# One block of a fused attention and feed-forward kernel: a maximum and its transpose taken one step earlier, four row transposes moved, clips interleaved

## The reference, cut to what matters

```
def _ln(x, g, b):                       # layer norm over the 512 features
    m = jnp.mean(x, axis=-1, keepdims=True)
    v = jnp.mean((x - m) ** 2, axis=-1, keepdims=True)
    return (x - m) * jax.lax.rsqrt(v + EPS) * g + b
h = _ln(x, pw_g[pathway_ids], pw_b[pathway_ids])
h = _ln(h, cp_g[compartment_ids], cp_b[compartment_ids])
t = _ln(x, tm_g[time_steps], tm_b[time_steps])
m, n, r = x + (one row each from three small conditioning networks)
s = _ln(x, ms_g[scale_type], ms_b[scale_type])
w = softmax(aw)
cat = concatenate([w[0]*h, w[1]*t, w[2]*m, w[3]*n, w[4]*r, w[5]*s])
u = _ln(silu(cat @ int_W1 + int_b1) @ int_W2 + int_b2, int_g, int_be)

def _L0_ffn_ref(lhs, rhs):              # lhs is u, rhs is 512 x 512
    lhs_scale = max(|lhs|, over a row) / 127
    rhs_scale = max(|rhs|, over a column) / 127
    q_lhs = clip(round(lhs / lhs_scale), -127, 127)
    q_rhs = clip(round(rhs / rhs_scale), -127, 127)
    return (q_lhs @ q_rhs) * lhs_scale * rhs_scale
out = x + _L0_ffn_ref(u, rhs)
```

## Time and profile before

| quantity | value |
|---|---|
| median of 3 runs | 1724.21 us (1722.79 to 1724.4) |
| the profiled execution | 1724.23 us |
| its span, first to last instruction | 1722.2 us |
| matrix engine busy | 1711.0 us, 99% |
| VectorE, ScalarE, POOL busy | 1249.2, 882.0, 728.7 us |
| granted clock of the matrix engine, mean | 0.998 |
| first block of the last stage | from 1208.65 to 1272.38 us of the span |

### The profile page before, as it was taken

One profiled execution on the slowest core, in us unless ns is written; L12 is line 12 of the kernel. 1 busy time (PEld: TensorE's weight loads), 2 busy tenths in 40 slices (PEclk: granted clock), 3 DMA queues, 4 the chain that ended last, 5 costly groups with the idle time before them and its releaser, 6 DMA issues. The chain is left out here.

```text
span 1722.2 us, 23029 instructions
## 1 busy us (share of the span) xinstructions
PE 1711.0 (99%) x7749; PEld 1385.2 (80%) x7749; DVE 1249.2 (73%) x1842; ACT 882.0 (51%) x1306; POOL 728.7 (42%) x642
## 2 busy tenths in 40 slices
PE   9999999999999999999999999999999999999998
PEld 7888888888888888888888888778787787787776
DVE  7766776658989688687464434447998988888876
ACT  7655556556666576575553222233554444543533
POOL 1122221222677465656571000006656755855823
PEclk9999999999999999999999999999999999999999
DMA  6011101120233434232445666887635444535411
GB/s 211 1 49 50 49 0 49 49 74 25 98 123 105 164 99 147 86 120 89 171 147 191 205 213 212 318 297 257 223 116 156 114 139 146 152 104 163 137 43 61
DMA packets 119959, 221.94 MB, mean 129 GB/s; under 512 B 25442, under 2 KB 25890, under 8 KB 119860
## 3 DMA queue, kind: packets, MB, share of 16 engines
q1 hardware_dynamic: 94308, 161.99, 28.1%
q10 hardware_dynamic: 18384, 33.56, 6.1%
q0 software_dynamic: 7168, 25.17, 4.9%
HBM read 158.26 MB, written 58.75 MB: 126 GB/s over the span
## 5 line engine op out<-in xcount | busy, mean ns | idle before, releaser
L1082 PE MATMUL bank<-h_parts,mlp_w 128*128 128x512 f32 x2016 | 459.2, 389 | 0.6 <-ACT product_copy L1302 0.5
L1082 PEld LDWEIGHTS bank<-h_parts,mlp_w 128*128 128x128 f32 x2016 | 378.1, 188 | 80.4 <-ACT product_copy L1302 1.4
L359 PE MATMUL bank<-h_parts,gate_w 128*128 128x512 f32 x1536 | 351.1, 389 | 0.6 <-DVE h_parts L696 0.6
L359 PEld LDWEIGHTS bank<-h_parts,gate_w 128*128 128x128 f32 x1536 | 288.1, 188 | 61.9 <-issue 0.9
L2161 PE MATMUL bank<-operand_parts,int_w 128*128 128x512 f32 x1152 | 274.9, 394 | 0.1
L1147 PE MATMUL bank<-p_parts,mlp_out_w 128*128 128x512 f32 x1152 | 267.4, 391 | 0.0
L2161 PEld LDWEIGHTS bank<-operand_parts,int_w 128*128 128x128 f32 x1152 | 213.7, 188 | 49.4 <-issue 4.8
L1147 PEld LDWEIGHTS bank<-p_parts,mlp_out_w 128*128 128x128 f32 x1152 | 214.6, 188 | 48.0 <-issue 3.4
L1423 POOL TENSOR_TENSOR product_out<-product_out,gelu 128x512 f32<-128x512 f32 x69 | 119.7, 1755 | 95.9 <-DVE product_out L1582 95.4
L621 POOL TENSOR_TENSOR decay_sq<-decay 128x512 f32<-128x512 f32 x32 | 39.2, 1226 | 278.8 <-DVE decay L709 278.8
L1302 ACT ACTIVATE product_copy<-bank,vec_sb 128x512 f32<-128x512 f32 x144 | 99.0, 687 | 106.3 <-PE bank L1082 105.5
(11 more groups left out here) (322 smaller groups left out, 2733.5 us busy)
## 6 DMA issues: line engine op xcount, KB each, us to landing
p_tile<-p_d ACTq DMA_DIRECT2D x96, 256.0 KB, 4.9
p_d<-product_out SPq DMA_DIRECT2D x92, 256.0 KB, 2.0
raw_mlp_w<-mlp_gate_g SPq DMA_DIRECT2D x21, 512.0 KB, 3.7
raw_mlp_w<-mlp_fc_g SPq DMA_DIRECT2D x21, 512.0 KB, 4.1
xin<-xT SPq DMA_DIRECT2D x8, 1024.0 KB
hs_d<-u SPq DMA_DIRECT2D x8, 1024.0 KB, 5.0
hs_pair<-hs_d SPq DMA_DIRECT2D x8, 1024.0 KB, 7.6
x_columns<-xT SPq DMA_DIRECT2D x8, 1024.0 KB, 6.9
```

The costliest lines, as they stand in the source:

```text
L359: i = pe.matmul(bank[:], gw[:, w, s, k, m * P:(m + 1) * P], hr[:, q, t, k, :], start=k == 0 and n == 0, stop=k == KT - 1 and n == 2)
L1082: i = pe.matmul(bank[:], wb[g % 2][:, s, w, kk, :], hop[u % 2][o][:, t, kk, :], start=first and kk == 0 and n == 0, stop=kk == 1 and n == ...
```

## The change

In the first block of the last stage: item 8 (the transposed maximum) goes ahead of step 9 where it stood behind it; VectorE's `rhs_maximum` goes between low parts 8 and 9 where it stood behind gain product 11; `last_tokens([2, 3])` goes ahead of step 6 where it stood behind it; and each of the four `rhs_clip` instructions follows one low part of the hidden layer, where all four stood ahead of the first low part. No instruction is added or removed.

```
+    first_peak = next(x for x in first_order if x[0] == "item" and items[x[1]][0:2] == ("qt", 0))
+    first_order.remove(first_peak)
+    first_order.insert(first_order.index(("main", 9)), first_peak)
...
         def item(b, q, n, prev, nxt):
-            elif not prev and n == XF:
-                pe.wait_ge(S["op_low"], 2 * XF)
-                last_tokens([2, 3])
...
         def body(b, q, prev, nxt):
             for what, n in order if prev else first_order:
                 if what == "main":
+                    if not prev and n == 6:
+                        pe.wait_ge(S["op_low"], 2 * XF)
+                        last_tokens([2, 3])
...
-        def hidden(b):
+        def hidden(b, prev):
             for m in range(KT):
                 dve.wait_ge(S["z_high"], KT * b + m + 1)
                 dve.tensor_tensor(zr[:, 1, m, :], tf[:, m % 2, :], zr[:, 0, m, :].bitcast(F32),
                                   ALU.subtract).then_inc(S["z_low"], 1)
+                if not prev:
+                    rhs_clip([m])
...
             front_low(0, 8)
+            rhs_maximum()
             front_low(0, 9)
             gain_product(0, 10)
             gain_product(0, 11)
-            rhs_maximum()
             front_low(0, 10)
             front_low(0, 11)
             rhs_peak()
...
             for k in range(KT):
                 split_second(k)
-            rhs_clip(range(0, 2))
-            rhs_clip(range(2, KT))
...
-            hidden(b)
+            hidden(b, prev)
```

## The result

22 runs each: 1726.74 us after the change against 1724.54 before. The ratio is 1.0014, with a 95% interval of 1.0008 to 1.002; that is +2.4 us (+1.4 to +3.4); the medians themselves are 2.2 apart. The profiled execution's span is 1723.1 us, 0.9 over that of before, but it came to step 4 of this block 1.13 us earlier (1221.11 against 1222.24), so its total says little. The two differ at the start of the span: from 14 to 16 us the granted clock is 0.50 in the profile of before and 1.00 in that of after. Seven of the fourteen profiles of this case have this fall, and step 4 starts at 1222.24 or later in them; the other seven have none, and it starts at 1221.14 or earlier. I therefore measure a stretch from here on: from the start of step 4 of the first block to the start of the next block's step 0.

A forecast was written before the change was run, and what follows sets the result against it. The matrix engine, busy 99% of the span, was taken as the bound, so its gaps count. +1.69 (the 0.80 already spent) - 0.46 = +1.2 us; 1724.23 + 1.23 = 1725.5 us, range 1722.3 to 1727.2.

The forecast's parts named there:

- The rows' transposes: Ahead of step 6: four gain items take 0.44 us instead of 1.24, so step 7 starts 0.80 us earlier.
- The maximum: First on VectorE, it makes gain product 10 and the peak's reduction late; item 12 starts at 1244.19, +1.69 us.
- the collisions: VectorE instructions with two SBUF inputs and POOL's tensor_tensor don't run together, so maxima and low parts alternate with POOL.
- The clips: Second layer: one clip behind each low part readies the third low part earlier, removing the matrix engine's wait, -0.46 us.
- The clock: Matrix engine behind the 3.1 us gap ahead of item 12: no clock loss in the sum; 1.7 us only as a rival.
- second rival: The 3.1 us gap ahead of item 12 also lowers the granted clock: +2.9 us, 1727.2 us; chance 0.11.
- the release: The peak's reduction on VectorE ends at 1244.14 and lets item 12 start on the matrix engine at 1244.19.
- VectorE behind the reduction: VectorE's lateness after the peak's reduction: no term in the sum; over 1.3 us later would lose the clips' gain.
- The first rival: No collisions with POOL, the maximum is quick: item 12 at 1241.70, -1.3 us, 1723.0 us; chance 0.27 with both forms.
- the prediction's own signs: Granted clock below 1 between 1244 and 1250 means the second rival; `second` ending about 1.2 us later means the forecast.

The follow-up runs named there:

- the added matmuls: Changed kernel with eight matmuls filling the gap ahead of item 12: stretch 52.46 us, ratio 1.0013; with POOL's third tile also cut, 51.22 us, 1.0007.
- the last kernel: Rows and clips moved, maximum in old place, items 12 and 13 behind step 10, low parts of steps 12 and 13 earlier on VectorE: 50.65 us, 1.0012 against before.

## Why the prediction was right, and where it was off

- *The rows' transposes, -0.80.* Right as a term: 0.44 for the gain items. Right too that it is spent ahead of item 12; alone it is worth 0.02.
- *The maximum, +1.69.* Measured +1.75. The chain of gain product 10, ScalarE and low part 11 came within 0.1 us of the forecast at each station, and the collisions fell as laid out. That they are what makes it late, cutting POOL's two tiles shows.
- *The clips, -0.46.* The mechanism was right, the size not: 0.76 alone, 0.83 in the whole. I read the idle time of the row; the distance between starts, which I had used for the gain items, would have shown it (11.71 for 48 matmuls where it now is 10.88).
- *The clock, given nothing in the sum.* This is the term that failed. The prediction had it as its second rival, at 0.11 and 1.7 us, because the other short gaps of the kernel had cost next to none. It cost 1.50 here. The errors of the terms close: +0.06 for the release, +1.50 for the clock, -0.37 for the clips, together +1.19, and the stretch is 1.20 over the forecast of +1.23.
- *VectorE behind the reduction, given nothing either.* The prediction followed VectorE to the release of item 12 and counted its lateness only against the clips' gain. VectorE came 3.58 us late to the low part of step 14, and with the clock whole the matrix engine waits for it: 52.46 us. So nearly all of the 1.50 would have been lost without the clock's fall too (52.46 us against 52.57).
- *The first rival*, no collisions, is refuted for this kernel and reproduced with POOL cut (48.83 us).

The measured time, 1726.74, lies in the range, but that is in part luck. It is 1.2 over the forecast, at the very end of what the forecast allowed by itself (1724.6 to 1726.7), and near the second rival's 1727.2. By the prediction's own signs it is the second rival that came: the granted clock was below 1 between 1244 and 1250 by the clock of before (in the profile after, 0.50 from 1244 to 1246), and `second` ended 2.4 us later, not 1.2. The mechanism of the release was right. The range held the result because it reached up to a rival that had been given one chance in nine.

## What to carry to other kernels

Moving an instruction earlier on one engine makes what it jumps over late; follow that through every engine to the thing that is released, and count each meeting of a two-input VectorE instruction with POOL as up to one POOL instruction more (0.6 to 1.25 us here, with POOL's at 1.3). Then follow the late engine past that thing, to the next one that waits for it. A wait that opens a gap on the matrix engine can cost clock on top, 1.5 to 1.7 us a time in these kernels whether the gap was 1.6 or 3.3 us long. The distance between two starts around the changed stretch shows both where single executions' totals don't. When removing one cause changes nothing, remove both before calling it innocent.

## What the runs showed of the hardware

- A `tensor_scalar` of four columns in SBUF took 1.95 us where it took 0.52 before. It started at 1243.10, within POOL's indirect DMA (from 1242.72), and ended at 1245.05 with POOL's product (1245.01). With POOL's first two tiles cut it took 1.01 and again ended with the product. With the third tile's product cut to 8 columns it took 0.21, though it ran within the same indirect DMA (1243.11 within 1242.73 to 1243.73). So it is the product that held it and not the DMA. The Trainium skill, SBUF — State Buffer, "Who interferes with whom", counts `tensor_scalar` among the instructions that can contend with GpSimd for the shared pair. The trace agrees, and adds that four columns wait as long as 512. The same section lets the earlier issue go first. Here the product's recorded start (1243.73) is 0.63 behind that of the instruction that it held, as with low part 11 before; why is open.
- The granted clock fell to 0.50 behind gaps between starts of 3.3 us (three kernels), 2.5 (two) and 1.6 (one). It stayed at 1.00 behind another of 1.7 (the kernel with the rows alone), behind two of 1.6 ahead of the added matmuls, and behind a wait of 2.17 (the last kernel). Waits of 1.12 and 2.01 were followed by a fall, waits of 1.16 and 2.17 were not, each in a single execution: in these kernels the length of the gap alone did not decide it.
